# The last four blocks of cross attention in eight consecutive slots, in buffers of both kinds, and the expert tiles dealt anew

## What is computed

```
x = _layernorm(x + _attn(x, x, x, sa_..., True), ln1_g, ln1_b)
x = _layernorm(x + _attn(x, encoder_output, encoder_output, ca_..., False), ln2_g, ln2_b)
x = _layernorm(x + _moe(x, router_w, router_b, e_w1, e_b1, e_w2, e_b2), ln3_g, ln3_b)
# _attn: 16 heads of 8 features, scores / sqrt(8), softmax, times V, times wo
# _moe:  router softmax, the 2 best of 8 experts with softmax weights;
#        each expert: gelu(x @ w1 + b1) @ w2 + b2, with 512 hidden features
```

## Time and profile before

| | |
|---|---|
| three timed executions | 770.77 to 774.32 us, median 773.73 us |
| the profiled execution, span | 818.8 us |
| PE busy, all matmuls | 601.7 us, 73% |
| DVE, ACT, POOL busy | 60%, 54%, 45% |
| mean granted TensorE clock | 0.878 |
| moved by DMA | 124.64 MB, mean 152 GB/s |

### The profile page before, as it was taken

How to read it: one execution, slowest core, us unless ns; L and a number is a source line. 1 busy time by engine, 2 the same in 40 slices (tenths; PEclk the granted TensorE clock), 3 DMA queues, 4 the chain that set the end, 5 groups by cost and what they waited for, 6 DMA issues and landing times. The chain is left out here.

```text
span 818.8 us, 21239 instructions
## 1 busy us (share of the span) xinstructions
PE 601.7 (73%) x7870; PEld 476.9 (58%) x7870; DVE 489.2 (60%) x1337; ACT 439.9 (54%) x814; POOL 369.8 (45%) x576
## 2 busy tenths in 40 slices
PE   2689687657667898877798776777767778588780
PEld 1356455445445676765676565667656667478570
DVE  4488998769987777786676677342465420402134
ACT  1246455335434599976797676555744454244120
POOL 7133443424348344427653572771654752600620
PEclk9989977879968899998998999799888789799886
DMA  4463445663224564544554454665544468588421
GB/s 111 113 207 95 140 131 171 203 194 105 59 82 133 167 177 143 171 142 136 158 167 130 124 155 137 199 197 167 157 127 149 135 214 260 163 266 261 147 62 32
DMA packets 141413, 124.64 MB, mean 152 GB/s; under 512 B 12224, under 2 KB 123600, under 8 KB 141312
## 3 DMA queue, kind: packets, MB, share of 16 engines
q1 hardware_dynamic: 134496, 113.06, 45.8%
q0 software_dynamic: 4368, 9.05, 3.8%
q10 hardware_dynamic: 2448, 1.18, 0.5%
HBM read 86.81 MB, written 38.54 MB: 153 GB/s over the span
## 5 line engine op out<-in xcount | busy, mean ns | idle before, releaser
L1727 PE MATMUL bank<-w_in,w_hl 128*128 128x128 f32 x704 | 109.2, 302 | 1.5 <-issue 1.3
L1172 DVE TENSOR_REDUCE row_max<-bank 128x16 bf16<-128x1024 f32 x64 | 78.2, 1223 | 49.0 <-PE bank L1589 48.2
L1727 PEld LDWEIGHTS bank<-w_in,w_hl 128*128 128x128 f32 x704 | 95.8, 210 | 1.9 <-issue 1.4
L966 ACT ACTIVATE probT<-bank 128x1024 f32<-128x1024 f32 x64 | 65.5, 1023 | 56.8 <-PE bank L1613 39.7
L836 POOL TENSOR_TENSOR veps<-mv,eps 128x1 f32<-128x1 f32 x64 | 15.7, 246 | 170.6 <-DVE mv L1210 170.6
L850 POOL TENSOR_TENSOR prob_lo<-probT,prob_hi 128x384 f16<-128x384 f32 x64 | 67.7, 1057 | 51.2 <-ACT prob_hi L969 50.7
L1713 PE MATMUL bank<-xT,w_in 128*128 128x128 f16 x1056 | 81.4, 231 | 2.9 <-issue 2.9
L1018 ACT ACTIVATE w_hl<-bank 128x512 f32<-128x512 f32 x88 | 52.5, 597 | 55.6 <-PE bank L1713 35.8
L875 POOL DMA_INDIRECT w_hl<-ys,pos x52 | 52.0, 999 | 49.9 <-DMA ys<-w_hl 34.8
L1713 PEld LDWEIGHTS bank<-xT,w_in 128*128 128x128 f16 x1056 | 69.6, 104 | 3.9 <-issue 3.8
L859 POOL DMA_INDIRECT xs<-x_hl,pos x60 | 62.8, 1047 | 17.7 <-issue 17.7
(11 more groups left out here) (182 smaller groups left out, 1581.0 us busy)
## 6 DMA issues: line engine op xcount, KB each, us to landing
w_in<-w_scr SPq DMA_DIRECT2D x96, 512.0 KB
q_scr<-q_hl SPq DMA_DIRECT2D x64, 128.0 KB
k_scr<-k_hl SPq DMA_DIRECT2D x64, 128.0 KB
q_st<-q_scr SPq DMA_DIRECT2D x32, 256.0 KB, 2.9
k_all<-k_scr SPq DMA_DIRECT2D x128, 64.0 KB, 2.2
xs_tile<-xs SPq DMA_DIRECT2D x42, 128.0 KB
ys<-w_hl SPq DMA_DIRECT2D x42, 128.0 KB
xs<-xs_tile SPq DMA_DIRECT2D x3, 1472.0 KB, 6.9
```

The costliest lines, as they stand in the source:

```text
L966: act.activation(probT[u.buf][:, :, :].rearrange("p h q -> p (h q)"), bank[:, KEYS:KEYS + 2, :].rearrange("p a n -> p (a n)"), ACT.Exp, sc ...
L1172: dve.reduce_max(row_max[u.buf][:, :], bank[:, SC:SC + 2, :].rearrange("p a (h k) -> p (a h) k", k=S), AX.X).then_inc(max_done[a], 1)
L1727: last = pe.matmul(expert_y(x), hid[x.par][:, c, :], w2_t[x.wb][:, c, :], start=False, stop=c == FC - 1, skip_group_check=True)
```

## The change

Cross attention of blocks 12 to 15 moves to slots 56 to 63, one unit in each (`DENSE_FROM`, `cross_slot`); everything up to slot 50 stands as before. The last cross unit is in slot 63, before in 71, and the program ends with slot 90, before 100.

Their q, k and v are now prepared two slots apart, the turning of the input and the projection of q in one slot (`crossed_at`: slots 52, 54, 56, 58; k and v in 53, 55, 57, 59). Blocks 12 to 15 no longer share the two buffers of cross attention: block 12 takes cross buffer 0, block 13 self buffer 0, block 14 self buffer 1, block 15 cross buffer 1 (`home`), and whoever fills one waits for its last tenant (`lived_there`). ACT waits in those slots for q as well before it copies the turned input.

Because they are derived from the last cross slot, the slots of what follows move too. A tile is a tail tile from the slot after the last unit on (`LAST_UNIT`, 63), before from the slot after ATTENTION_END on (now 69, before 77):

| | before | now |
|---|---|---|
| tiles in slots 56 to 63 | 13 | 8, one a slot |
| first tail tile, of tiles 0 to 87 | 57 (third chunk) | 33 (second chunk) |
| tail tiles | 31 | 55 |
| route steps, chunk 3 and chunk 4 | slots 72 to 74, 76 to 78 | 66 to 68, 68 to 70 |
| scatters of chunk 3 | 3 a slot, from 75 | 8 a slot, 69 and 70 |
| rows of blocks 3 to 6 gathered | slots 67, 69, 71, 73 | 68, 70, 71, 72 (as `at_end`) |
| first tile of the last tiled chunk | slot 83 | slot 73 |

One tile more is done before slot 56 (two tiles in slot 51). POOL's wait at the end covers the older output semaphores too, since blocks of both sorts now mix otherwise.

```diff
-LAG = 2
+DENSE_FROM = 11
...
+def cross_slot(b):
+
+    return 4 * b + 10 if b <= DENSE_FROM else 4 * DENSE_FROM + 10 + 2 * (b - DENSE_FROM)
...
+        if slot - cross_slot(b) in (0, 1):
+            return Unit(CROSS, Block(b), slot - cross_slot(b))
+    return None
...
+def crossed_at(b, d):
+
+    if b <= DENSE_FROM:
+        return 4 * b + (4, 6, 7)[d]
+    return cross_slot(b) - (4, 4, 3)[d]
...
+def home(a, b):
+
+    if a == CROSS and b.n > DENSE_FROM:
+        return ((CROSS, 0), (SELF, 0), (SELF, 1), (CROSS, 1))[b.n - DENSE_FROM - 1]
+    return a, b.par
+
+
+def lived_there(a, b):
+
+    if a == CROSS and b.n > DENSE_FROM:
+        return ((CROSS, Block(NBLK - 6)), (SELF, Block(NBLK - 2)), (SELF, Block(NBLK - 1)), (CROSS, Block(NBLK - 5)))[b.n - DENSE_FROM - 1]
+    return (a, b.back(2)) if b.back(2).exists() else None
...
 def last_cross(c):
-    return 4 * (FIRST_BLK[c] + CHUNK[c] - 1 + LAG) + 3
+    return cross_slot(FIRST_BLK[c] + CHUNK[c] - 1) + 1
...
-ATTENTION_END = last_cross(CHUNKS - 1) + 6
+LAST_UNIT = last_cross(CHUNKS - 1)
+ATTENTION_END = LAST_UNIT + 6
...
-        self.tail = TILE_SLOT[m] > ATTENTION_END
-        self.settled = m >= 2 and TILE_SLOT[m - 2] > ATTENTION_END
+        self.tail = TILE_SLOT[m] > LAST_UNIT
+        self.settled = m >= 2 and TILE_SLOT[m - 2] > LAST_UNIT
...
-    return GROUP_SLOT[f] >= ATTENTION_END
+    return GROUP_SLOT[f] >= ATTENTION_END - 1
...
             def fetch_q(a, b):
 
                 sp.wait_ge(q_out[a], b.times(32, 32))
-                if b.back(2).exists():
-                    sp.wait_ge(st_ready[a], b.back(2).times(2, 2))
-                sp.dma_start(q_st[a][b.par][:, :, :], q_scr[a][b.par].rearrange("(g p) r t -> (p r) g t", g=G)).then_inc(
+                if had := lived_there(a, b):
+                    sp.wait_ge(st_ready[had[0]], had[1].times(2, 2))
+                a2, p2 = home(a, b)
+                sp.dma_start(q_st[a2][p2][:, :, :], q_scr[a][b.par].rearrange("(g p) r t -> (p r) g t", g=G)).then_inc(
...
             for p in range(2):
+                pool.wait_ge(*stored(next(f for f in reversed(range(NBLK)) if f % 2 == p and not at_end(f))))
                 pool.wait_ge(*stored(NBLK - 2 + p))
...
-                if s == 0 and ca.exists():
+                if ca:
                     act.wait_ge(inT_ready[CROSS], ca.times(1, 1))
+                    if ca_q:
+                        act.wait_ge(q_ready[CROSS], ca_q.times(1, 1))
```

More of the change, by code:

```diff
@@ L127, in unit_at, with crossed, cross_tokens_at @@
             return Unit(SELF, Block(b), slot - self_slot(b))
-    blk = Block(t - LAG)
-    return Unit(CROSS, blk, s % 2) if s >= 2 and blk.exists() else None
+        if slot - cross_slot(b) in (0, 1):
[5 more added lines that the diff above has]
+    return cross_slot(b) - (4, 4, 3)[d]
+def crossed(slot, d):
+    return next((Block(b) for b in range(NBLK) if crossed_at(b, d) == slot), None)
+def cross_tokens_at(slot):
+    return next((Block(b) for b in range(1, NBLK) if (crossed_at(b - 2, 0) if b > 1 else 0) == slot), None)
+def home(a, b):
[6 more added lines that the diff above has]
+    return (a, b.back(2)) if b.back(2).exists() else None
 def prepared_at(b, d):
@@ L732, in slot @@
                     send_k(SELF, self_b)
[L733 to L736, removed]
+                if cross_q:
+                    send_q(CROSS, cross_q)
+                if cross_k:
+                    send_k(CROSS, cross_k)
                 if (c := chunk_closes(g)) is not None:
@@ L754, in slot @@
                     fetch_k(SELF, self_b)
[L755 to L758, removed]
+                if cross_q:
+                    fetch_q(CROSS, cross_q)
+                if cross_k:
+                    fetch_k(CROSS, cross_k)
                 by_weights, by_rows = asked_at_open(g)
@@ L956, in v_high @@
                     r = slice(64 * h, 64 * h + 64)
-                    last = act.activation(v_hi[a][b.par][r, :, h, :, 0:HD], v[r, :, :, :], ACT.Copy)
+                    last = act.activation(v_hi[a2][p2][r, :, h, :, 0:HD], v[r, :, :, :], ACT.Copy)
                 last.then_inc(v_hi_ready[a], 1)
@@ L1092, in slot @@
                     act.wait_ge(v_ready[SELF], sa.times(1, 1))
-                if s == 2 and ca.exists():
-                    high(CROSS, ca, q_ready, q_hi, q_hl, bq, q_out)
+                if ca_q:
+                    high(CROSS, ca_q, q_ready, q_hi, q_hl, bq, q_out)
                 if sa:
                     v_high(SELF, sa)
[L1097 to L1100, removed]
+                if ca_k:
+                    act.wait_ge(v_ready[CROSS], ca_k.times(1, 1))
+                    high(CROSS, ca_k, k_ready, k_hi, k_hl, bk, k_out)
+                    v_high(CROSS, ca_k)
                 if (u := unit_at(g - 5)) and u.kind == CROSS:
@@ L1407, in low_parts @@
                 sa = prepared(g, 2)
-                if s == 2 and ca.exists():
+                if ca_q:
                     if sa:
                         dve.wait_ge(v_hi_ready[SELF], sa.times(1, 1))
-                    low(CROSS, ca, q_hi, q_lo, q_hl, bq)
+                    low(CROSS, ca_q, q_hi, q_lo, q_hl, bq)
                 if sa:
                     v_low(SELF, sa)
-                if s == 3 and ca.exists():
-                    dve.wait_ge(v_hi_ready[CROSS], ca.times(1, 1))
-                    low(CROSS, ca, k_hi, k_lo, k_hl, bk)
-                    v_low(CROSS, ca)
+                if ca_k:
+                    dve.wait_ge(v_hi_ready[CROSS], ca_k.times(1, 1))
+                    low(CROSS, ca_k, k_hi, k_lo, k_hl, bk)
+                    v_low(CROSS, ca_k)
             def slot(g):
@@ L1512, in found_at @@
                 def found_at(q, k):
-                    t, s = divmod(q, 4)
-                    ca = Block(t - 1)
-                    if s == 0 and ca.exists():
+                    if (ca := crossed(q, 0)) and not crossed(q, 1):
                         return inT_done[CROSS], ca.times(1, 1)
@@ L1815, in slot @@
                     sa = None
-                if sa or s == 0 and ca.exists():
+                if sa or ca:
                     row_free(g)
```

69 lines of the change are left out of this document (34 added, 35 removed).

## The result

Four executions of the changed kernel took 746.25 to 756.12 us, median 749.99; four of the kernel before, on the same chip, 770.77 to 774.32, median 772.40. The ratio is 0.971 (0.966 to 0.976): 22.4 us less, where 29.7 had been forecast.

A forecast was written before the change was run, and what follows sets the result against it. Taken as bound by latencies between engines, PE in the middle, busy 73% of 818.8 us. Terms of 240.7 us replaced 272.0 us, giving 787.5 us profiled; times 0.945, 744 us (own range 732 to 758, 8 in 10: 720 to 766).

The forecast's parts named there:

- Dense slots, 75.2 us: Slots 56 to 63, one tile each with chunk 2 routed and scattered: 75.2 us, taken from slots 40 to 47.
- One tile moved, 3.6 us: A second tile in slot 51 costs 3.6 us, the usual tile spacing; lower bound nothing.
- 32 tail tiles, 84.5 us: The next 32 tail tiles, 9 of the second and 23 of the third chunk, at the steady 2.64 us: 84.5 us.
- a seam, 6.1 us: Routing and the change of chunk among the 32 tail tiles add 6.1 us, once, over the steady price.
- POOL's runs, 1.8 us: 16 scatters and then 8 gathers in a row on POOL make PE stand inside tiles: 1.8 us.
- Last 23 tiles, 69.5 us, and what follows, 65.3 us, as now: The last 23 tiles and the stretch after the last tile keep their order: 69.5 us and 65.3 us, unchanged.
- Scaling by 0.945: Timed executions are 0.945 of the profiled one (773.73 / 818.8); the same share turns 787.5 us into 744 us.
- Edits at nothing: New buffers, ACT's wait for q, POOL's added wait at the end and routing of chunk 3 cost nothing.
- All steady: Rival: seams and bursts hide, all 55 tail tiles at 2.64 us; 48 us less, 728 us; chance 22%.
- PE's own length: Rival: tail tiles at 2.00 us each, transfers never binding; 83 us less, 695 us; chance 3%.
- Little gained: Rival: dense slots at 11.5 us, 32 tail tiles at 3.40 us; 4 us more, 777 us; chance 6%.
- q and k late: Rival: blocks 12 to 15 each reach their scores a slot late, 37.6 us on top, 780 us; chance 7%.

The follow-up runs named there:

- second profile: The kernel before, unchanged, profiled again: 769.74 us, span 768.0 us.

## Why the prediction was nearly right

*Dense slots, 75.2 us.* Right in size and half right in cause. Seven of them took 69.6 us; eight tiles, from the gelu of tile 24 to that of tile 32, 74.6. ACT was named as what they can't carry, and POOL; it was DVE and then POOL, shown by the kernel that routed elsewhere (52.0 us). The row borrowed was itself too long: slots 40 to 47 took 75.2 us in the first profile and 69.5 us in the second and in the changed kernel, and a dense slot is 1.3 us dearer than those. Two errors against each other.

*One tile moved, 3.6 us.* Slot 51 with two tiles took 10.1 us after and 7.6 before: 2.5 us, within the bounds of nothing and 3.6.

*32 tail tiles, 84.5 us, and a seam, 6.1 us.* The steady price was right (2.64 forecast, 2.71 measured), the seam wasn't where it was put: 31 spacings in 83.9 us hold two routings and a change of chunk. The row of 27.2 us that gave it was misread. From gelu to gelu the same eight spacings, tile 56 to 64, took 24.4 us in the first profile and 23.0 in the second; 2.8 us of the row lie outside of them. What stands out in both profiles is the opening of the tail, 5.2 and 4.8 us from the gelu of tile 56 to that of 57. The changed kernel has such an opening too, the 9.7 us from tile 32 to 33, 7.0 over the steady price. No term of the sum names it.

*POOL's runs, 1.8 us.* This failed at its root. The row was read rightly but was no property of the kernel; behind the same gathers PE worked 7.70 and 8.53 of 10 us in the second profile of before. In the changed kernel, among the 16 scatters in a row and the first gathers behind them:

```profile
605.00:615.00 10.00, 7.79 (x102) 7.45 (x101) 1.22 (x7) 6.55 (x14) 7.88 (x10) 1.00 0.88 270
```

The rule that was weighed against this term made it zero: the Trainium skill, SBUF — State Buffer, Who interferes with whom, says that a DMA never contends with a compute engine. These rows agree with it. What stopped PE in the first profile stays open.

*Last 23 tiles, 69.5 us, and what follows, 65.3 us, as now.* Nearly right that they would not change (59.2 and 59.4 us for the last tiled chunk from its first gelu; 51.2 and 53.9 behind it). Wrong in size: the first profile had 67.1 and 65.7 us for the same two, 8 and 14.5 more than the second, which were that execution's.

*Scaling by 0.945.* Tiles 25 to 64 with the dense slots were summed to 75.2 + 84.5 + 6.1 + 1.8 = 167.6 us; from the gelu of tile 24 to that of tile 64 they measured 168.3, without any factor. That this is so close is in part luck: the seam and POOL's runs, 7.9 us, weren't there, and the opening of the tail, 7.0 us, wasn't in the sum. The old stage, 198.7 us from gelu to gelu in the first profile, was 181.3 in the second. The 50.8 us between the two profiles weren't spread evenly: 11.4 lie in the 484 us ahead of tile 24, 17.4 between tiles 24 and 64, 7.5 from there to tile 87 and 14.5 in the 66 us behind. One factor for both made the old stage 0.945 x 198.7 = 187.8 us, 6.5 too long, and the new one 158.4, 9.9 too short: 29.4 us less in this stage, where the traces show 13.0. In all, 744 us were forecast and 750 measured, a gain of 29.7 us forecast; the traces differ by 13.7, the medians by 22.4, since the trace after is of the slowest of its executions. The mechanism was right, the direction and the range too; the size of the old stage was off, and the tail's price per tile, which the prediction named as the first suspect, was not. An extra 45 us over the timed median should have been a reason to doubt single stretches, not to scale them all.

*Edits at nothing.* Borne out: no wait at the scores though SP's longest for a low part is 8.1 us (`q_hl`, 6.7 in the earlier trace rows), PE once 3.0 us for such a part at a projection (L1603), routing of chunk 3 done 30 us ahead of the gelu of its first tile (last scatter 610.8, gelu 641.0).

*The rivals.* "All steady" had the inside of the tail right. Its terms for tiles 25 to 87, 75.2 + 145.2 = 220.4 us, measured 231.3; 7.0 of the difference are the opening of the tail, most of the rest its price, 2.72 in place of 2.64. Its total was wrong because it took the seams and bursts from a baseline that doesn't have them either. PE's own length didn't come: 2.70 us with the transfers at 270 GB/s. Half the weights still bought only 0.37 us a tile. The Trainium skill, DMA: Bandwidth & Descriptors, Where 436 GB/s comes from, has a core's HBM limit at about 358 GB/s. The ten microseconds from 650.6 us of the changed kernel had 301 GB/s, and none of the stretches shown here has more. "Little gained" would have needed 3.40 us a tile; the kernel without the tail banks had 3.17 over tiles 33 to 57. "q and k late" is refuted by the absence of its wait, and by the kernel that gave these blocks their usual buffers and lost nothing.

## What to carry to other kernels

Profile the kernel before twice before pricing a change from its rows: where the profiled execution is longer than the timed ones, the excess lies in some stretches and not in all, and a common factor shifts the forecast. Where several engines share a slot, a change is worth what it takes from the engine whose list ends last there; here a tile more in a dense slot cost some 0.3 us, and a tile less was paid in the tail at 1.8 to 3.1 us. Work moved to a later stretch with idle engines is free only if no queue holds something urgent behind it, as ACT's store of block 10 held PE for 12.4 us: look for the store or the root that will stand ahead.

## What was not expected

One execution of an unchanged kernel was 818.8 us long where all others are 768 to 777, with PE standing inside tiles (4.29 of 10 us busy). It was the first profile taken; none of the 13 later ones shows such a pause. Halving the bytes of the weights, 256 KB less for each tile, took only 0.37 us off a tile in the last tiled chunk, though the DMA engines were at 0.88.
